# A graph layer on one core: odd batches gathered four batches ahead instead of six, and the pausing memset behind the first 176 early gathers only

## The reference, cut to what matters

```python
def _L0_gnn_ref(node_states, edge_features, ..., from_idx, to_idx):
    edge_in_f = concatenate([node_states[from_idx], node_states[to_idx], edge_features], axis=-1)
    msgs_f = _mlp2(edge_in_f, W1_f, b1_f, W2_f, b2_f)
    agg = segment_sum(msgs_f, to_idx, num_segments=n_nodes)
    edge_in_r = concatenate([node_states[to_idx], node_states[from_idx], edge_features], axis=-1)
    msgs_r = _mlp2(edge_in_r, W1_r, b1_r, W2_r, b2_r)
    agg = agg + segment_sum(msgs_r, from_idx, num_segments=n_nodes)
    node_in = concatenate([agg, node_states], axis=-1)
    return node_states + _mlp2(node_in, Wn1, bn1, Wn2, bn2)
h = maximum(_layernorm(x, axis=-1), 0.0)
x = x + _L0_gnn_ref(h, edge_attr_64, ..., src, dst)
```

## Time and profile before

| | us |
|---|---|
| median of 3 runs | 1609.94 (1607.84 to 1611.34) |
| profiled execution | 1610.51 |
| its span, first to last instruction | 1608.8 |
| GpSimd busy | 1103.2 (69%) |
| TensorE busy | 1280.4 (80%), mean granted clock 0.858 |

### The profile page before, as it was taken

One profiled execution on the slowest core, in us unless ns is written; L12 is line 12 of the kernel. 1 busy time (PEld: TensorE's weight loads), 2 busy tenths in 40 slices (PEclk: granted clock), 3 DMA queues, 4 the chain that ended last, 5 costly groups with the idle time before them and its releaser, 6 DMA issues.

```text
span 1608.8 us, 29477 instructions
## 1 busy us (share of the span) xinstructions
PE 1280.4 (80%) x7070; PEld 970.6 (60%) x7070; DVE 972.0 (60%) x3294; ACT 942.1 (59%) x2256; POOL 1103.2 (69%) x1003
## 2 busy tenths in 40 slices
PE   5899998457877778887787877778888756899998
PEld 4677777335655555665565656556666544666665
DVE  7999999426666666666666666666666641222222
ACT  4888888345555555555545555555555524677776
POOL 7888888888888888888888888888888761000000
PEclk9999999768788887778778788887777887999999
DMA  6899998425555555555555555555555547999998
GB/s 214 288 312 315 312 316 290 141 51 111 109 111 111 111 105 104 104 105 105 104 104 105 105 102 100 103 103 103 104 102 101 101 71 235 345 353 343 347 342 298
DMA packets 238410, 281.00 MB, mean 175 GB/s; under 512 B 53170, under 2 KB 155200, under 8 KB 238348
## 3 DMA queue, kind: packets, MB, share of 16 engines
q1 hardware_dynamic: 168408, 241.57, 45.2%
q0 software_dynamic: 68992, 38.59, 20.5%
q10 hardware_dynamic: 948, 0.30, 0.1%
HBM read 162.62 MB, written 117.72 MB: 174 GB/s over the span
## 4 chain that ended last, share of the span: by engine, by line
POOL 33%; issue 22%; DMA 15%; PE 4%; DVE 3%; ACT 1%; POOLq 0%; SPq 0%; DVEq 0%; ACTq 0%
POOL table L532 28%; DMA out_x<-ncentred 12%; POOL got_odd L514 6%; DMA table<-to_send,scatter_at 2%; DVE ncentred L1138 2%; DVE same L979 1%; PE bank L833 1%; PE bank L871 1%; DMA same<-table 1%; PE bank L820 1%; PE bank L882 0%; PE bank L818 0%; SPq L392 0%; PE bank L804 0%; PE bank L892 0%
## 5 line engine op out<-in xcount | busy, mean ns | idle before, releaser
L532 POOL DMA_INDIRECT table<-to_send,scatter_at x392 | 622.6, 1588 | 134.0 <-issue 118.4
L846 PEld LDWEIGHTS bank<-message,same 128*128 128x128 f32 x1960 | 270.3, 222 | 44.2 <-issue 39.2
L846 PE MATMUL bank<-message,same 128*128 128x128 f32 x1960 | 290.9, 313 | 4.8 <-DVE message L1011 4.8
L639 ACT ACTIVATE nh<-nx,all_sums,all_rstd 128x64 f32<-128x64 f32 x784 | 280.2, 434 | 0.1
L514 POOL DMA_INDIRECT got_even<-in_x,gather_first x196 | 212.9, 1086 | 39.8 <-issue 34.7
L775 PE MATMUL bank<-wn_h,nturned 128*128 128x256 f32 x784 | 196.7, 394 | 31.7 <-ACT nhidden L683 24.1
L514 POOL DMA_INDIRECT got_odd<-in_x,gather_at x180 | 180.2, 1001 | 54.9 <-issue 54.0
L804 PE MATMUL bank<-ident,h_ends 128*128 128x128 f32 x196 | 52.0, 359 | 198.7 <-DVE h_ends L1020 192.6
L979 DVE TENSOR_SCALAR_CACHE_REDUCE same<-others,ids 128x128 f32<-128x128 int32 (+3 forms) x392 | 190.7, 543 | 12.7 <-issue 7.9
L818 PE MATMUL bank<-turned,w_ends 128*128 128x256 f32 x392 | 167.1, 516 | 37.9 <-ACT turned_edge L609 37.9
L775 PEld LDWEIGHTS bank<-wn_h,nturned 128*128 128x128 f32 x784 | 143.1, 192 | 67.9 <-issue 36.2
(11 more groups left out here) (79 smaller groups left out, 1984.3 us busy)
## 6 DMA issues: line engine op xcount, KB each, us to landing
nx<-in_x SPq DMA_DIRECT2D x194, 256.0 KB
table<-nhidden SPq DMA_DIRECT2D x97, 512.0 KB
same<-table SPq DMA_DIRECT2D x97, 512.0 KB, 5.4
others<-numbers SPq DMA_DIRECT2D x196, 128.0 KB
out_x<-ncentred SPq DMA_DIRECT2D x97, 256.0 KB, 4.4
nx<-out_x SPq DMA_DIRECT2D x55, 256.0 KB, 4.8
out_x<-nh SPq DMA_DIRECT2D x31, 256.0 KB
table<-to_send,scatter_at POOLq DMA_INDIRECT x392
```

Source lines behind the costliest of these rows:

```text
L532: pool.indirect_dma_start(table, bass.IndirectOffsetOnAxis(ap=scatter_at[s][:, k:k + 1], axis=0), to_send[s][:, k, :], None, compute_op=AL ...
L639: last = act.activation(nh[s][:, g, :], nx[place][:, g, :], ACT.Relu, bias=all_sums[:, at, g:g + 1].rearrange("p a g -> p (a g)"), scale=a ...
L846: last = pe.matmul(bank[6 + s][:, k * M:(k + 1) * M], same[s][:, o, k * P:(k + 1) * P], message[s][:, o, :], start=(o == k), stop=(o == KB ...
```

## The change

LOOK goes from 3 to 2. Two odd batches instead of three are gathered early, the loop starts with pair 2 instead of pair 3, and each odd batch b is gathered behind the scatters of batches b - 5 and b - 4 instead of b - 7 and b - 6. The memset stands behind the first 176 of now 204 early gathers instead of behind all 208, and ScalarE's first copy waits for these 176.

```diff
@@ -90,7 +90,8 @@
     RING = 4
-    LOOK = 3
+    LOOK = 2
+    PAUSED = 176
     EARLY = 4
@@ -562,6 +563,8 @@
                         gather(got_odd[i][:, 0, :], at, s_got[i], [k])
                     else:
                         continue
+                    if pauses == PAUSED:
+                        continue
                     if pauses:
                         pool.wait_ge(s_paused, pauses)
                     pool.memset(idle, 0.0).then_inc(s_paused, 1)
@@ -621,7 +624,7 @@
                 elif s == 0:
-                    act.wait_ge(s_paused, KB * (PAIRS + LOOK))
+                    act.wait_ge(s_paused, PAUSED)
                 act.copy(to_send[s][:, :, :].rearrange("p k m -> p (k m)"), bank[6 + s][:, :]).then_inc(s_send[s], 1)
```

## The result

The changed kernel took 1881.0 us (median of 4 runs, 1866.7 to 1886.6), the kernel before in the same session 1608.9 us (1607.7 to 1611.3). The ratio is 1.1675, with a 95% interval of [1.1609, 1.1742]: about 17% slower, 272 us. The prediction was 1889 us. Five executions in runs 1, 3 and 7 to 9 took 1.7 to 3.3% longer than the fastest of their kernel; the ratios given leave these out, the medians don't.

A forecast was written before the change was run, and what follows sets the result against it. The prediction took GpSimd's instruction stream to set the time of the edge part. It summed 1610.5 - 12.6 (early gain) + 47 x (4.2 + 2.0) (loop waits) to 1889 us, about 17% slower, range 1785 to 1990.

The forecast's parts named there:

- The chain of a round: In the batch loop, GpSimd waits for its own gather through VectorE and ScalarE: 4.2 us lost, 47 times.
- e + 4.52: Predicted start, in us, of scatter b - 3 in a round; e is the end of the second gather.
- the landing: From a gather's end until VectorE can use its rows: 1.75 us taken, 0.85 us as low end.
- The odd scatter: In the loop, scatter b - 2 waits for TensorE's join: between 0.2 and 3.8 us by clock, 2.0 us taken.
- Both terms together: Loop loss of even and odd scatters over 47 rounds: 47 x (4.2 + 2.0) = 291 us.
- The other signs: GpSimd's scatter idle time some 400 us; VectorE's odd-batch centring waits for gathers; TensorE's edge-part clock below 0.8.
- The four gathers at the end: Early gathers moved behind scatters 92 and 93, covered by a landing wait: no cost, 5.2 us if uncovered.
- The early gain: Before scatter 0, fewer early gathers and memsets save 12.6 us, lower bound 5.9 us.
- Rival 1: TensorE's clock always comes back early in the loop: 207 us lost, time 1805 us; chance 0.22.
- rival 2: TensorE's clock stays low through each pair's first join: 376 us lost, time 1974 us; chance 0.21.
- rival 3: Not slower: GpSimd never waits in the loop, only the early gain is left, 1598 us; chance 0.05.
- rival 4: Loop stall partly absorbed, with a landing of 0.85 us and an early clock: 165 us, time 1763 us; chance 0.05.

The follow-up runs named there:

- run 1: Changed kernel with the memset behind all 204 early gathers: 1886.4 us; kernel before with it behind only the first 176 of 208: 1612.7 us.
- 3: Changed kernel with each half of an odd batch gathered one scatter earlier, behind scatters b - 6 and b - 5: 1611.9 us, ratio 1.0022.
- 7 to 9: Kernel before with memsets behind only the first 144 or 64 early gathers, half as wide, or behind every second: 1663.9, 1756.4, 1797.2, 1800.1 us.
- run 4: Changed kernel with ScalarE's copy to to_send placed ahead of the square: 1865.5 us, ratio 1.1598.
- Run 5: Changed kernel with extra identity transposes on TensorE ahead of each even batch's transposes: 1871.0 us with 72, 1810.1 us with 92.
- run 2: Changed kernel with all four gathers of odd batch b behind scatter b - 5, none behind b - 4: 1712.2 us, ratio 1.0636.
- run 6: Changed kernel with memsets behind all early gathers again, the last 28 into a tile of their own: 1879.0 us, ratio 1.1676.
- the kernel with 64 pauses: Kernel before with the memset behind only the first 64 of the 208 early gathers: 1756.4 us, ratio 1.0934.

## Why the prediction was right, point by point

**The chain of a round** (gather, centring, square, copy, scatter b - 3): right. The rows show it link by link, run 1 puts it on the distance alone, run 4 on the square ahead of the copy. Its size was 3.88 us for 4.2 predicted (e + 4.16 in the round shown, for e + 4.52), and the difference is mostly the landing: 1.52 us (1.50 in the mean of the 47 rounds) for the 1.75 I took from the scatters, still well above the low end of 0.85. The Trainium skill, "DMA: Bandwidth & Descriptors", section "Anatomy of one DMA — SWDGE (gpsimd) path", gives about 2.0 us; the trace has 1.52 us from the end of the issue and 2.51 from its start (876.36 to 878.87).

**The odd scatter** (b - 2): 2.16 us for 2.0. The middle that I took between 0.2 and 3.8 turned out as a real mixture: 17 of 47 near nothing, 22 over 2.5 us. The round with the late clock starts its scatter at e + 18.5 (920.32, with e = 901.83), just as worked out from the earlier trace rows; the one with the early clock starts at e + 14.5, held by GpSimd's own queue, where I had 14.7, to within the 0.14 us that it lost. Run 5 shows that this term goes when the clock stays high. The Trainium skill, "TensorE: Matmul & The Clock Gate", section "HAM oscillation — how this bites in real kernels", has every tile start throttled when its wait is long enough; here every pair starts at 0.50. What decides between the early and the late return after equal idle times of about 10 us no run shows; that part of the forecast was a middle between two bounds, not knowledge, and that 2.16 came out so near to 2.0 is luck.

**Both terms together**: 284 us of loss for 291 predicted. The other signs came too: the idle time at the scatters (412.8 us for some 400), VectorE's wait for the gathers, and a mean granted clock of 0.73 from 332 to 1608 us, against 0.80 before.

**The four gathers at the end**: next to no cost of their own, right. Behind scatters 92 and 93 they stand where GpSimd waited for landings, 4.6 us in all beyond the 0.30 us of issue, for some 5.2 us of issue.

**The early gain**: the term that was mis-sized. I took 12.6 us, with 5.9 as lower bound; it was 8.3. GpSimd's part was right, the gathers did end at 326.70 and 1.26 us apart. What failed was "scatter 0 follows the last gather by 0.30 us": I took the copy to be released at about 292 and to be done, and did not ask what else it waits for between 292 and 326. It was TensorE's join, whose signal came at 330.91. In the profile before, ScalarE's wait of 38.6 us covers whatever else would be late there. The mis-sizings, 4.3 us less gain against some 12 us less loss up to scatter 97 and 1.5 us behind it, partly cancel: 1889 against 1880.6.

**The rivals.** Rival 1 is refuted by the 22 rounds over 2.5 us, rival 2 by the 17 rounds near nothing, rival 3 by the 64 waits for `to_send`, and rival 4 by the landing of 1.52 us.

## What to carry to other kernels

A prefetch distance has a step, not a slope: list in program order what stands between the issue of a load and its first reader on every engine, and look for the landing that the reader waits for anyway. Five batches ahead cost 0.2% here and four cost 17%: with five VectorE waited up to 2.8 us for its rows, with four up to 11.4, more than the 7.8 us by which the copy behind it was early, and then the reader's queue held the loader. Work that stands between two dependent transfers is cover for their landing, so moving it (run 2) can cost as much as what it was moved for. A pause that looks like waste may set a pace that others need: making each of them 0.11 us shorter (memsets of 220 ns instead of 329) cost 12%.

## What the runs showed that was not expected

GpSimd's indirect gathers, issued closely enough, hold the other engines: at 61 in 100 us next to nothing is seen, at 70 and 71 ScalarE waits up to 23 and 29 us and at 77 some 31 us in a window of the begin part, with inputs whose rows have ended. It isn't bandwidth, with 49 GB/s moved, nor instructions being loaded: in the kernel with 64 pauses no packet of the instruction queues falls into 150 to 250 us. What comes late are TensorE's signals. The trace has the time of a part of the semaphore signals: in that kernel, from 115 to 315 us, the 20 signals of VectorE and ScalarE come within 0.01 us of the end of their rows, while all 15 of TensorE come 8.7 to 61.8 us late; in the kernel before, from 20 to 285 us, none of TensorE's 131 is over 2.6 us late. The hold also outlasts the gathers: in the kernel with 64 pauses the last one ends at 295.88 and the last hold, 18 us long, ends at 312.49, and from 305 to 312 no queue moves anything. The late copy of the changed kernel is of this kind, as the signal that it waited for was TensorE's, 19 us late, and as it too follows gathers 1.26 us apart and ends 4 us behind the last; but there three signals of VectorE's are late too, by up to 5.4 us, and run 6 has such waits with gathers 1.45 us apart (its join's signal is 9.8 us late), so pace alone isn't shown to explain that one. Why the signals are late, and whether the matmuls are late themselves, whose ends in the rows are modelled, stays open.

TensorE's clock, after equal idle times of about 10 us, comes back in some rounds within 5 us of the start and in others after 9.4 to 12.8. In run 5 with 72 transposes it fell again in 32 of the 48 pairs, though TensorE had paused for only some 2 to 4 us.
